# Three moves in a linear-attention and FFN kernel: LayerNorm 2's last steps, copies of weight blocks, and the order of the gate's halves

## The reference, cut to what matters

```
xn = layernorm(x)
# attention branch
q, k, v = split(xn @ W_qkv.T + b_qkv);  q, k = elu(q) + 1, elu(k) + 1
kv  = einsum('bhnd,bhnv->bhdv', k, v);  k1 = k.sum(tokens)
out = (q @ kv) / clip(sum(q * k1), 1e-6)
out = layernorm(out @ W_proj.T + b_proj) * gamma + beta      # LayerNorm 2
attn = out + xn
# FFN branch; all weights are ternary, each followed by a scale
h = silu(xn @ w1) * (xn @ w2)
h = gelu(h @ h1);  h = gelu(h @ h2);  ffn = h @ w3
return x + attn + ffn
```

## Time and profile before

| what | value |
|---|---|
| median of 3 runs | 1481.9 us (1480.41 to 1482.11) |
| the profiled execution | 1483.11 us, its span 1481.0 us |
| PE busy | 1462.3 us (99%) |
| DVE busy | 1189.8 us (80%) |
| ACT busy | 926.1 us (63%) |
| POOL busy | 359.1 us (24%) |
| mean granted TensorE clock | 0.999 |

### The profile page before, as it was taken

The page is one execution under the profiler, slowest core; times in us unless marked ns, Lnnn a source line. Parts: engine busy times, 40 slices in busy tenths (PEclk is TensorE's granted clock), DMA queues, the critical chain, the costliest instruction groups (busy, mean ns, idle before and its releaser), DMA issues.

```text
span 1481.0 us, 33333 instructions
## 1 busy us (share of the span) xinstructions
PE 1462.3 (99%) x11020; PEld 1271.2 (86%) x11020; DVE 1189.8 (80%) x2208; ACT 926.1 (63%) x1727; POOL 359.1 (24%) x464
## 2 busy tenths in 40 slices
PE   9999999999999999999999999999999999999998
PEld 5988979979798897988979889798897979979797
DVE  6847978789787897978878788897878978789786
ACT  4555666766566675665756667566675666766564
POOL 2203214132140321303223041320413204132130
PEclk9999999999999999999999999999999999999999
DMA  8787845728366382764718548184481845727363
GB/s 236 234 287 246 295 139 198 245 88 284 112 228 216 118 286 77 242 207 145 271 61 274 180 146 306 35 287 161 163 280 51 291 141 196 246 88 264 127 202 114
DMA packets 89090, 287.66 MB, mean 194 GB/s; under 512 B 9696, under 2 KB 55392, under 8 KB 65760
## 3 DMA queue, kind: packets, MB, share of 16 engines
q0 software_dynamic: 43296, 231.75, 47.2%
q1 hardware_dynamic: 44928, 54.29, 11.2%
q10 hardware_dynamic: 832, 1.18, 0.2%
HBM read 270.42 MB, written 25.17 MB: 200 GB/s over the span
## 4 chain that ended last, share of the span: by engine, by line
PE 69%; DVE 10%; issue 10%; ACT 9%; DVEq 1%; ACTq 0%
PE ps L1032 38%; PE ps L1005 8%; PE ps L1003 7%; ACT values_out L1371 4%; PE ps L1067 4%; DVE partial_sums L1752 3%; PE ps L892 2%; ACT hidden_out L1348 2%; PE ps L955 2%; PE ps L944 2%; PE ps L893 2%; PE ps L894 2%; DVE zkv L1637 1%; ACT relu_tmp L1384 1%; ACT L1383 1%
## 5 line engine op out<-in xcount | busy, mean ns | idle before, releaser
L1032 PE MATMUL ps<-operands_a,hidden_weights 128*128 128x256 f32 x2520 | 348.6, 282 | 0.0
L1032 PE MATMUL ps<-lo_a_in_bits,hidden_weights 128*128 128x256 f16 x2520 | 323.5, 273 | 0.0
L1032 PEld LDWEIGHTS ps<-operands_a,hidden_weights 128*128 128x128 f32 x2520 | 317.8, 188 | 0.3
L1032 PEld LDWEIGHTS ps<-lo_a_in_bits,hidden_weights 128*128 128x128 bf16 x2520 | 241.1, 98 | 30.2
L783 POOL DMA_DIRECT2D hidden_weights<-weight_blocks x236 | 127.8, 541 | 566.4 <-PE ps L1032 539.0
L1702 DVE SCALAR_TENSOR_TENSOR lo_a_in_bits<-values_a,operands_a 128x512 f16<-128x512 f32 x315 | 214.8, 705 | 37.6 <-ACT operands_a L1343 26.5
L1709 DVE SCALAR_TENSOR_TENSOR lo_out_in_bits<-values_out,hidden_out 128x512 f16<-128x512 f32 x120 | 78.8, 688 | 103.8 <-ACT hidden_out L1348 103.8
L1005 PE MATMUL ps<-xnT,w_ffn 128*128 128x512 f32 x512 | 150.5, 421 | 0.0
L1032 PE MATMUL ps<-operands_b,hidden_weights 128*128 128x256 f32 x840 | 140.5, 289 | 2.0 <-DVE gate_ring L1752 1.9
L1343 ACT ACTIVATE operands_a<-values_a 128x512 fp32r<-128x512 f32 x180 | 111.3, 627 | 38.2 <-POOL values_a L758 17.4
L1297 ACT ACTIVATE gate_ring<-ps,vectors 128x512 f32<-128x512 f32 x128 | 85.9, 683 | 67.2 <-PE ps L1003 47.7
(11 more groups left out here) (165 smaller groups left out, 2839.1 us busy)
## 6 DMA issues: line engine op xcount, KB each, us to landing
hidden_weights<-weight_blocks POOLq DMA_DIRECT2D x180, 1024.0 KB, 5.3
hidden_weights<-weight_blocks POOLq DMA_DIRECT2D x60, 512.0 KB, 5.3
raw_weights<-weight_blocks SPq DMA_DIRECT2D x70, 231.5 KB, 4.4
hidden_weights<-in_w_ffn POOLq DMA_DIRECT2D x16, 512.0 KB, 8.4
weight_blocks<-weight_sums SPq DMA_DIRECT2D x16, 512.0 KB, 4.8
weight_blocks<-in_w_ffn SPq DMA_DIRECT2D x16, 512.0 KB, 11.0
out_dram<-acc SPq DMA_DIRECT2D x31, 256.0 KB, 2.2
x<-in_H SPq DMA_DIRECT2D x15, 512.0 KB, 6.5
```

The source lines that it names most:

```text
L1032: r = mm(bank[:, m * HT:(m + 1) * HT], wk, xk, start=i in firsts and begins and m == 0 and j == 0, stop=i in lasts and ends and m == 1 and ...
```

## The change

Five edits:

- In `body` on DVE, `ln2_gain_and_shift(t)`, `ln2_sum(t)` and `put_ones(t + 1)` now stand right behind `add_c21(t, 3)`, ahead of `check_piece(t - 1, 4)` and of the low parts of C21. Before, the three LayerNorm steps stood behind those low parts, right ahead of `z_step(t + 1, 0)`.
- In `body` on PE, `gate_group(t, 6)` stands ahead of `apply_kv(t, 0)` and `apply_kv(t, 1)`; `first_body` keeps its order.
- `LO_FIRST_GROUPS` goes from (1, 3, 6) to (1, 3, 5, 7), for all tiles.
- SP waits for the four stores of the last set of sums before it issues the first copy.
- `clear_low` on DVE, once in the program, fills `low` with two instructions in place of one.

```diff
-LO_FIRST_GROUPS = (1, 3, 6)
+LO_FIRST_GROUPS = (1, 3, 5, 7)
...
                 store_sums(3)
+                for n in range(4):
+                    sp.wait_ge(s_stored[SETS - 1][n], 16)
                 copy_blocks(0)
...
                     gate_group(t, 2)
+                    gate_group(t, 6)
                     apply_kv(t, 0)
                     apply_kv(t, 1)
-                    gate_group(t, 6)
                     gate_group(t, 3)
...
-                v.memset(low[:], 0).then_inc(s_low0, 1)
-                dve.wait_ge(s_low0, 1)
+                for cols in (slice(0, CHECK_COLS // 2), slice(CHECK_COLS // 2, CHECK_COLS)):
+                    v.memset(low[:, cols], 0).then_inc(s_low0, 1)
+                dve.wait_ge(s_low0, 2)
...
                     add_c21(t, 3)
+                    if more:
+                        ln2_gain_and_shift(t)
+                        ln2_sum(t)
+                        put_ones(t + 1)
                     if checking and more:
                         check_piece(t - 1, 4)
-                    if more:
-                        put_ones(t + 1)
                     lo_of_output(t, 0, "C21", first > 0)
                     lo_of_output(t, 1, "C21", first > 0)
                     if more:
-                        ln2_gain_and_shift(t)
-                        ln2_sum(t)
                         z_step(t + 1, 0)
```

## The result

The changed kernel takes **1484.2 us** (median of 20 runs, 1483.35 to 1485.54), the kernel before 1481.76 us beside it (20 runs, 1480.41 to 1483.08). The ratio is 1.0017, with a 95% interval of 1.0010 to 1.0024: a loss of 2.4 us, which is small (0.17%) but outside the interval of no change. The profiled execution took 1484.78 us, its span is 1482.6 us, the clock 1.000.

What follows compares the result with a forecast made beforehand. PE, busy 99%, was taken as the bound, with its waits. Span: 1481.0 - 14.4 (LayerNorm steps) + 17.4 (gate) - 0.7 (`w_out`) = 1483.3 us; the same +2.3 on the median gives 1484.2, own range 1482.4 to 1486.0.

Steps and rivals of the forecast that it cites:

- product 5: Gate's product 5: PE waits about 0.4 us more for the low part of G1's T1; tile 1.16 us late there.
- tile 15: The gate's cost of 1.16 us was counted in all 15 tiles that run `body`, this one included.
- `w_out`: First output group: load of `w_out` lands sooner without copies queued ahead, ending PE's 0.73 us wait; -0.7 us taken.
- The LayerNorm steps: Tile's end: steps moved into DVE's idle time end PE's waits for `zkv`; 1.03 us gained in each of 14 tiles.
- The gate's wait: Gate, place 7: PE waits 0.66 us for the bank that DVE's `gated` of place 4 frees.
- The collision of T2 with the low part of T1: Gate, G1: DVE's low part of T1 meets POOL's T2 and takes about 1.1 us where another takes 0.69.
- The period: Time of one tile in the loop: 0.1 us above that of the kernel before.
- The order of halves: Gate on PE: both orders take about 9.1 us, no gain; tile 0 bounds -0.2 and +0.2 us.
- the case of the bank waits alone: Rival: tile late by only 0.64 or 0.73 us in the gate, total 1476.4 to 1477.8 us; 22%.
- The second collision on PE's path: Slower rival: later POOL and DVE steps of G1 collide once more, 0.43 us in 15 tiles, 1490.7 us; 18%.

Runs made afterwards that it cites:

- the T2-as-zeros run: Changed kernel with POOL's T2 of G1 written as zeros by a memset but for two columns of each half, left out of the computation: 1479.11 us, ratio 0.9983.
- the run in which T2 waits: Changed kernel with one more wait on POOL, T2 of G1 starting only when DVE's low part of G1's T1 is made: 1503.41 us, ratio 1.0147.

## Why the prediction was right, point by point

- **The time**: 1484.2 predicted and measured; against the kernel before, +2.3 predicted and +2.4 measured. The loop came out by the mechanism that was forecast, 14 x 0.15 = 2.1 us for 1.8. That the totals agree to 0.1 us is luck: the terms for product 5, tile 15 and `w_out` were too large, others of 0.04 to 0.08 us a tile were left out, and these errors offset each other.
- **The LayerNorm steps, -1.03 us a tile**: right. 6.55 us from the output group to the gate where 6.54 was reckoned, and 13.9 us for this part alone where 14.4 was.
- **The gate's wait, 0.66**: right, 0.65 from start to start, with `gated` of place 4 ending at 862.31 where it would be 862.32 by the prediction's distance from place 4.
- **The collision of T2 with the low part of T1**: right. The low part takes 1.11 us where 1.12 was said, and the T2-as-zeros run takes it away. The step of the sum was 1.16 - 0.64 = 0.52; measured are 0.36 at product 5, and 0.08 at the first matmuls of product 1, which the prediction did not have. That 0.08 is one step that takes 0.20 us for 0.12; it is in each kernel that has both the later `apply_kv` and the new order of halves, and in none that has only one of them; its cause is open.
- **A longer wait for ACT's `relu_tmp`, not predicted**: with `zkv` early, `kv_step` 1 loses 0.04 us more than before (the row at 838.32).
- **The period, +0.13**: measured +0.15. The terms read in rows give -1.03 + 0.64 + 0.08 + 0.36 + 0.04 = +0.09; the other 0.06 is about what the order of halves costs by itself in small steps. By whole runs it is -1.01 for the LayerNorm steps alone (89.86), +0.04 for halves and copies on top of them (89.90), and +1.12 for the gate group (91.02).
- **Tile 15, +1.16**: not confirmed. From its gate to its last matmul the profiled executions show 85.31 for 85.08 us. Kernels in which the code there is that of before range from 84.50 to 85.24, the one that shares the changed kernel's shows 85.65, so a cost of some 0.1 to 1.1 us is possible, and the median has no room for more than a part of 1.16.
- **`w_out`, -0.7**: wrong. The step that failed took the 0.73 us of the earlier trace rows for something that each execution has, and took it off the median, where nothing shows that it was ever in. The load does land some 3 us sooner, but in every other profiled execution PE asks for it 10.4 us or more behind its issue, and the 9.0 to 9.5 us that it took there without the edit were already enough. Of the rule named there (the Trainium skill, "DMA: Bandwidth & Descriptors", section "Queues, rings and completion order"), the result that it was to give, no gain, came about, but not by the reasoning that the prediction drew from it: copies that were under way did hold the load up more than copies that start beside it, 9.0 to 9.7 us for 6.4 to 7.3. How the DMA engines shared their time in either case was not looked into, so this does not refute the turns themselves.
- **The order of halves, 0**: right for the gate (9.06 us) and for tile 0 (97.87 us for 97.85), but 0.06 us a tile come on top behind the gate. That is 0.8 us in 14 tiles, more than the 0.2 that the prediction allowed.
- **The rivals**: the case of the bank waits alone fell with the row at 869.62. The second collision on PE's path did not come here, but the run in which T2 waits shows that it was near: 1.85 us more on DVE opened a wait of 1.4. The Trainium skill's lock of the shared port ("SBUF — State Buffer", section "Who interferes with whom") agrees with each of the meetings seen: DVE's 1.11 and 1.62 us for 0.69 where POOL was first, and POOL's 1.50 for 1.28 where DVE was (the row at 878.21).

## What to carry to other kernels

Before a wait is removed or moved, ask what is queued behind it on the same engine: here a small step (`gated`) stood behind one that waits for the moved matmuls, and that alone was 8.6 of the 15.6 us that the move of the matmuls costs. Do the parts of a change one by one: the LayerNorm steps alone are 1.0% faster, and the rest of the change gives back all of it and 2.4 us more. And a stall that one execution shows once is no term of a sum until another execution shows it too.

## What the runs showed of the hardware

- A DVE instruction with two SBUF inputs that starts well inside a POOL subtraction ends 0.54 to 0.56 us behind POOL's end, whether it started 0.7 us into it (1.11 us at 868.45) or 0.24 (1.62 us at 880.49), each for 0.69.
- A load of 1 MB beside DRAM-to-DRAM copies of 512 KB takes 9.0 to 9.7 us when the copies have been under way for some 5 us, and 6.4 to 7.3 us when they start at about the same time.
- Before the first gate the program takes 19.4 to 20.6 us in the profiled executions, with the same code. The spans of two profiled executions can differ by 1 us for that alone, while their tile periods agree within 0.05 us in most tiles.
